# Attention units of 16 blocks, four exponentials in a row, and moved weight loads in a fused attention and feed-forward layer on eight cores

## The reference

```python
xn = _layernorm(x)                                  # x: 8 x 2048 x 1024
q, k, v = split(xn @ W_attn + b_attn)               # 16 heads of 64
att = q @ k.T / sqrt(64) / temperature + slope[h] * (pos_k - pos_q)   # causal
y = softmax(att) @ v
attn = y @ W_proj + b_proj
gate = xn @ (w_gate / 127).T                        # 3072 wide
up = xn @ (w_up / 127).T
ffn = (silu(gate) * up) @ (w_down / 127).T
out = x + attn + ffn
```

## Time and profile before

| | |
|---|---|
| median of 3 runs | 970.39 us (969.66 to 970.48) |
| the profiled execution | 968.67 us |
| its span on the slowest core (core 3) | 967.1 us (cores 958.5 to 967.1) |
| TensorE busy (x6272) | 905.9 us, 94% |
| VectorE busy | 498.7 us, 52% |
| ScalarE busy | 503.1 us, 52% |
| GpSimd busy | 300.5 us, 31% |
| mean granted TensorE clock, core 3 | 0.987 |

### The profile page before, as it was taken

The page is one execution under the profiler, slowest core; times in us unless marked ns, Lnnn a source line. Parts: engine busy times, 40 slices in busy tenths (PEclk is TensorE's granted clock), DMA queues, the critical chain, the costliest instruction groups (busy, mean ns, idle before and its releaser), DMA issues.

```text
span 967.1 us, 18777 instructions; the slowest of 8 cores (958.5 to 967.1 us)
## 1 busy us (share of the span) xinstructions
PE 905.9 (94%) x6272; PEld 407.4 (42%) x6272; DVE 498.7 (52%) x1110; ACT 503.1 (52%) x603; POOL 300.5 (31%) x296
## 2 busy tenths in 40 slices
PE   3999999999999999999999999979937999999998
PEld 1444344444444444444444444434413444444443
DVE  4650577777777777777777777766201011110111
ACT  3754677776787787787776877666323100000000
POOL 1010233323432324233324233345624233211220
PEclk9999999999999999999999999989978999999999
DMA  8842279999999999999899999999997837352221
GB/s 259 263 139 81 52 147 234 183 204 219 211 212 208 177 221 220 198 225 211 155 225 202 193 204 200 199 219 216 277 308 247 269 103 263 107 190 72 87 87 43
DMA packets 333341, 182.15 MB, mean 188 GB/s; under 512 B 303680, under 2 KB 315968, under 8 KB 329664
## 3 DMA queue, kind: packets, MB, share of 16 engines
q1 hardware_dynamic: 327776, 164.13, 76.2%
q0 software_dynamic: 2304, 8.39, 2.8%
q10 hardware_dynamic: 3168, 8.44, 2.3%
HBM read 84.46 MB, written 20.97 MB: 109 GB/s over the span
## 4 chain that ended last, share of the span: by engine, by line
PE 76%; DMA 6%; issue 6%; SPq 5%; DVE 4%; ACT 2%; POOL 1%; DVEq 0%; ACTq 0%; POOLq 0%
PE ps_r L911 25%; PE ps_dn L1003 17%; PE ps_r L894 11%; PE ps_s L963 7%; PE ps_dn L1010 6%; PE ps_y L978 5%; PE ps_r L934 4%; DMA xstage<-xin 3%; DMA late_i<-wd_r 2%; DVE sc L670 2%; SPq L388 2%; ACT pr L824 1%; SPq L471 1%; DVE st L617 1%; DMA stage_i<-wd_r 1%
## 5 line engine op out<-in xcount | busy, mean ns | idle before, releaser
L824 ACT ACTIVATE pr<-sc,cm 128x2048 bf16<-128x2048 f32 (+15 forms) x256 | 290.7, 1197 | 57.4 <-DVE cm L670 57.3
L670 DVE CUSTOM_DVE_ANT_0 sc<-ps_s,ramp 128x1024 f32<-128x1024 f32 (+7 forms) x256 | 243.8, 988 | 95.3 <-PE ps_s L963 80.5
L911 PE MATMUL ps_r<-xnT,wubuf 128*128 128x512 bf16 x768 | 206.9, 384 | 18.0 <-ACT gh_s L747 15.3
L911 PE MATMUL ps_r<-xnT,wgbuf 128*128 128x512 bf16 x768 | 204.8, 381 | 1.4 <-ACT gh_s L747 1.4
L1003 PE MATMUL ps_dn<-wdres,hb 128*128 128x512 bf16 x768 | 169.5, 381 | 5.0 <-DVE hst L698 5.0
L548 POOL TENSOR_SCALAR th_s<-th_s 128x512 f32<-128x512 f32 x96 | 59.3, 617 | 289.0 <-ACT th_s L745 288.9
L670 DVE CUSTOM_DVE_ANT_0 sc<-ps_s,ramp,cm 128x1024 f32<-128x1024 f32 (+7 forms) x128 | 99.9, 815 | 54.1 <-PE ps_s L963 53.5
L721 DVE SCALAR_TENSOR_TENSOR outsb<-ps_dn,xres 128x512 f32<-128x512 f32 x32 | 20.7, 687 | 202.9 <-PE ps_dn L1010 182.3
L894 PE MATMUL ps_r<-xnT,wqk_b 128*128 128x512 bf16 x512 | 120.9, 380 | 0.3 <-ACT gh_s L747 0.3
L554 POOL TENSOR_TENSOR gs_s<-th_s,gh_s 128x512 bf16<-128x512 f32 x96 | 111.2, 1159 | 26.2 <-POOL th_s L548 24.0
L1003 PEld LDWEIGHTS ps_dn<-wdres,hb 128*128 128x128 bf16 x768 | 75.4, 98 | 97.0 <-issue 7.4
(11 more groups left out here) (48 smaller groups left out, 530.7 us busy)
## 6 DMA issues: line engine op xcount, KB each, us to landing
stage_i<-wg_r SPq DMA_DIRECT2D x24, 512.0 KB, 4.6
stage_i<-wu_r SPq DMA_DIRECT2D x24, 512.0 KB, 5.6
h_sc<-hst SPq DMA_DIRECT2D x96, 128.0 KB, 2.4
late_i<-wd_r SPq DMA_DIRECT2D x9, 1024.0 KB, 9.0
hb<-h_sc SPq DMA_DIRECT2D x3, 3072.0 KB, 16.0
xstage<-xin SPq DMA_DIRECT2D x16, 512.0 KB, 6.5
stage_f<-wqk_r SPq DMA_DIRECT2D x8, 1024.0 KB, 6.1
xres<-xin POOLq DMA_DIRECT2D x16, 512.0 KB, 4.8
```

The lines of the kernel that those rows point to most:

```text
L670: e.tensor_tensor_reduce(scores(n, g + (2 if b == 2 else 0), c0, w), ps_s[:, g * 1024:g * 1024 + w], ramp[:, T - wide + c0:T - wide + c0 + ...
L824: e.activation(pr[n % 3][:, b0 * 128:(b0 + blocks) * 128], scores(n, r, 0, blocks * 128), AF.Exp, bias=cm[:, at:at + 1], scale=-1.0).then_ ...
L911: mm = e.matmul(ring(what, f), w[:, dc * 128:(dc + 1) * 128], xnT[:, dc * T + tb * 512:dc * T + tb * 512 + 512], start=(dc == 0), stop=(dc ...
```

## The change

It does five things.

1. **Units.** A pair has nine units instead of eight: (14,0), (13,1), ... (8,6) with 16 blocks a head, then row 15 alone (16 blocks) and row 7 alone (8 blocks). A unit has two steps of 1024 keys: the first 1024 of the long row, then the rest of the long row together with the short row in one filling of `ps_s`; row 7 has one step. That is 17 steps a pair instead of 24.
2. **ScalarE.** All four exponentials of a unit stand at the very start of ScalarE's work for the unit's last step, ahead of the Q or K copy and of the tanh of the gate products that end in that step.
3. **Weights.** The chain is split in two: gate and up through `stage_i`, and Q, K and the early down chunks, in halves of 512 KB, through `stage_f` and `stage_d`. Both stay in SyncE's queue.
4. **The end.** 92 pairs lie in the steps and 4 follow. h is collected in five `hst` buffers instead of four; the load of h for the first four row blocks and the first three late chunks are issued earlier; the late weights and the h block exchange their places in SBUF, and the three first late chunks all go to ScalarE behind the tanh of the last three gate products.
5. **The start.** Five small VectorE instructions on constants move from before the third to behind the fifth block of x; the first Q and K weights get a buffer of their own.

The core of the diff:

```diff
-NU = 8 * NHP
+UNITS = [(14 - j, j) for j in range(7)] + [(15,), (7,)]
+NUP = len(UNITS)
+NU = NUP * NHP
-NF_ATT = 88
+NF_ATT = 92
+NHS = 5
...
+    i, j = rows
+    return [[(0, 0, 1024)], [(0, 1024, (i - 7) * 128), (1, 0, (j + 1) * 128)]]
...
-    n, b = divmod(k, 3)
+    n, b = STEPS[k]
     n -= LAG
-    return [[(n, 0)], [(n, 1), (n, 2), (n, 3)], []][b]
+    rows = [(n, r) for r in range(2 * len(UNITS[n % NUP]))]
+    if b == 0 and not last_of(k):
+        return rows[:1]
+    return rows[1:] if b else rows
...
             for k in range(NST):
-                if k < NSB and qk_at(k) is not None:
+                n, b = STEPS[k]
+                if k < NSB and last_of(k):
+                    for r in range(2 * len(unit_of(n)[2])):
+                        weights(n, r)
+                if qk_at(k) is not None:
                     evac_qk(*qk_at(k))
                 for f in ended(k, "g"):
                     tanh_gate(f)
-                if k < NSB and k % 3:
-                    for r in range(2):
-                        weights(k // 3, r + (0 if k % 3 == 1 else 2))
...
             for f in ended_late("g"):
                 tanh_gate(f)
-                if f == NF_ATT + t:
-                    convert_late(t)
-                    t += 2
+                if f >= NF - 3:
+                    convert_late(f - NF + 3)
...
             for i in range(4, NT + 1):
...
+                if i == 5:
+                    e.wait_ge(sem["l_const"], 16 * 4)
+                    e.tensor_scalar(t8_s[:, :], temp_s[:, :], 8.0, None, AluOpType.mult).then_inc(sem["v_t"], 1)
```

More of the change, by code:

```diff
@@ new lines, in y_at, with y_block, batches_of @@
+def y_at(x):
+    return sum(len(rows) for rows in UNITS[:x])
+def y_block(tt):
+    return [i for rows in UNITS for i in rows].index(tt)
+def batches_of(x):
+    rows = UNITS[x]
+    if rows == (15,):
+        return [[(0, 0, 1024)], [(0, 1024, 1024)]]
+    if rows == (7,):
+        return [[(0, 0, 1024)]]
+    i, j = rows
+    return [[(0, 0, 1024)], [(0, 1024, (i - 7) * 128), (1, 0, (j + 1) * 128)]]
+STEPS = [(n, b) for n in range(NU) for b in range(len(batches_of(n % NUP)))]
+NSB = len(STEPS)
@@ new lines, with last_of @@
+STEPS += [(n, b) for n in range(NU, NU + LAG) for b in range(2)]
+NST = len(STEPS)
+def last_of(k):
+    return k + 1 == NST or STEPS[k + 1][0] != STEPS[k][0]
+SUMS = [(k, seg, g) for k in range(NSB) for seg in range(len(batches_of(STEPS[k][0] % NUP)[STEPS[k][1]]))
+        for g in range(2)]
+SUM_AT = {what: o for o, what in enumerate(SUMS)}
+ROW_AT = {}
+for _k, _seg, _g in SUMS:
+    _n, _b = STEPS[_k]
+    ROW_AT[_n, 2 * batches_of(_n % NUP)[_b][_seg][0] + _g] = SUM_AT[_k, _seg, _g]
+EXPS = [(n, r) for n in range(NU) for r in range(2 * len(UNITS[n % NUP]))]
@@ L200, in extra_loads, with late_done @@
 def extra_loads():
-    out = {}
+    items = {}
     for p in range(2, NHP):
[L205 to L209, removed]
+        f = FM[FIRST_OF[NUP * (p - 2)]] // 16 + 1
+        f += (1 - f) % 4
+        items[f], items[f + 2] = ("q", p, 0), ("q", p, 1)
+    f = FM[FIRST_OF[NUP * (NHP - 1)]] // 16 + 1
+    f += (1 - f) % 2
     for c in range(3):
-        out[f + 4 * c] = ("d", c)
-    return out
+        items[f + 4 * c], items[f + 4 * c + 2] = ("d", c, 0), ("d", c, 1)
+    return items
 EXTRA = extra_loads()
[L218 to L241, removed]
+EXTRAS = [("q", 1, 0), ("q", 1, 1)] + [EXTRA[f] for f in sorted(EXTRA)]
+NEARLY = sum(1 for what in EXTRAS if what[0] == "d") // 2
 NLATE = HCP - NEARLY + 4
+LATE_ON = ["a", "a", "a"] + ["ga"[t % 2] for t in range(NLATE - 3)]
+def late_done(t):
+    return f"{LATE_ON[t]}_lw", LATE_ON[:t + 1].count(LATE_ON[t])
 def build_program(T):
@@ L329, in build_program @@
             sd = [sb(first, f"sd{i}", [128, 1], F32) for i in range(4)]
+            wq_f = sb(first, "wq_f", [128, 2048], F32)
             rs = [sb(first, f"rs{i}", [128, 1], F32) for i in range(4)]
-        sc = sb(st, "sc", [128, 2 * 17 * 128], F32)
+        sc = sb(st, "sc", [128, 2 * 16 * 128], F32)
+        with contextlib.ExitStack() as late:
+            hb0 = sb(late, "hb0", [128, HCN * 512], BF16)
+        pr = [sb(st, f"pr{i}", [128, 32 * 128], BF16) for i in range(3)]
         with contextlib.ExitStack() as late:
@@ L1030, in _ @@
                     for half in range(2):
+                        if hc == 0 and tt == 2:
+                            if half == 0:
+                                e.wait_ge(sem["v_y"], NU)
+                            else:
+                                e.wait_ge(sem["v_h"], NF)
                         down(tt, hc, half)
```

418 lines of the change are left out of this document (205 added, 213 removed), and 4 rows, old and new, of the table SEMS.

## The result

| | before | after |
|---|---|---|
| median | 970.43 us (969.66 to 971.13, 4 runs) | 1050.24 us (1045.61 to 1051.85, 4 runs) |
| ratio, 95% interval | | 1.0815 (1.0778 to 1.0851) |
| profiled execution, its slowest core | 967.1 us (core 3) | 1047.6 us (core 2) |
| TensorE busy / idle in that span | 905.9 / 61.2 us | 924.4 / 123.2 us |
| granted clock, that core | 0.987 | 0.956 |

The change costs 8%, 80 us. The direction was forecast, the size was not: 1015 us was said, and 1050 lies outside the range of 986 to 1034. All medians and ratios leave out the runs in which one die held a much lower granted clock than the other, and in e13 and e14, where cores 4 to 7 held 0.98 in every run, cores 0 to 3 are compared.

What follows compares the result with a forecast made beforehand. The order of TensorE's instructions was taken as the bound; -11.2 - 35.4 - 5.2 + 1 + 69.4 + 8.6 + 18 = +45.2 on the 970.4 us median gave 1015 us (own range 1003 to 1027, eight in ten 986 to 1034).

Steps and rivals of the forecast that it cites:

- ScalarE's exponentials first, +69.4: Attention: tanh behind four exponentials frees gate banks late, TensorE stands; 69.4 us lost (55 to 77).
- its 0.3 a place: Method's excess at two observed places of the kernel before; 0.3 x 24 taken from 76.6, leaving 69.4 us.
- the eleven places: Gate ends within three matmuls of the scores, bank wanted in the same step: TensorE waits 43.2 us in all.
- the thirteen: Places where a Q or K product heading the next step wants the gate's bank: 29.0 us in all.
- The place worked out as 4.5: Example gate product: bank wanted at T + 3.2, free at T + 7.7 us, so TensorE stands 4.5 us.
- The clock, +18, with 5.2 of before gone: Eleven long stalls each bring half clock, 1.65 us apiece, +18 (0 to 24); earlier clock losses of 5.2 us vanish.
- The rival "more": Waits of 2.3 to 2.5 us drop the clock too, narrow scores cost, down waits: 1027 to 1036 us, chance 0.10.
- The whole 35.4 us of before come off: TensorE's earlier waits in and after the attention, 16.7 + 11.1 + 5.0 + 2.6 us, all vanish: -35.4.
- The 14.0 at the end: TensorE's wait until 724.49 us, late chunks and SyncE's queue delaying a tanh; said to vanish, within the 35.4.
- the 5.0 for cm at 633: Wait in the attention put down to the single chain of weights; splitting the chain removes 5.0 us.
- VectorE's waits, +8.6: Up products' banks come free after sums and division; TensorE waits in eleven units, +8.6 us (3 to 12).
- The groups of scores, -11.2: Score groups in the attention fall from 24 to 17 a pair, 56 x 0.20 us: -11.2 (8 to 12).

Runs made afterwards that it cites:

- e13: e2 with five of the six early down-chunk half loads cut to 16 columns of 1024, same instructions and order: 942.1 us, ratio 0.9694.
- e14: e2 with one wait added: in a unit's last step ScalarE does nothing before the step's first sum is there: 952.3 us, ratio 0.9788.
- e12: Changed kernel with tanh and copy of the eleven longest-waited gates ahead of the four exponentials, all others behind: 981.6 us, ratio 1.0098.
- e10: Changed kernel with 22 unread matmuls of 248 columns ahead of each of the eleven longest-waiting gate products only: 1024.8 us, ratio 1.0555.
- e2: Changed kernel with the tanh of gates ending within a last step's first nine gate and up matmuls ahead of the exponentials, later ones behind: 942.7 us, ratio 0.9676.
- e3: Kernel before, with only the four exponentials of a unit put first in ScalarE's work for the unit's third step: 987.0 us, ratio 1.0141.
- e4: Changed kernel with unread matmuls, 22 ahead of each of eleven gate products and 10 ahead of thirteen shorter-waiting products: 1017.1 us, ratio 1.0455.

## Why the prediction was wrong

Its sum of +45.2 us, term by term against what the runs showed:

- **ScalarE's exponentials first, +69.4.** Right in mechanism, place and count: 78.2 us in 32 pieces of up to 4.5, where 25 to 35 of up to 4.2 were said. The sum before its 0.3 a place was taken off, 76.6, was nearly exact: 43.2 were worked out for the eleven places and 29.0 for the thirteen, and the rows have 43.9 and 29.4. The place worked out as 4.5 measured 4.38 as the profile counts idle time, and 4.54 from when the matmul could have begun (184.71) to 189.25; at the two places of before, too, 0.16 us of what the method was too high by lies in this way of counting. +9 us.
- **The clock, +18, with 5.2 of before gone.** This is the step that failed most. The net was +12.8 and the trace shows +26. Two parts of it were wrong. The eleven long waits were given 1.65 us each; e12 has 24.9 / 11 = 2.3, since behind several of them the clock stayed at 1.2 GHz for twice as long, as in 237.8 to 244.6; its own hold such a price, 0.17 x 20 = 3.4 us in the stretch of the one wait of 5.0. And the thirteen waits of 1.5 to 2.9 us were given nothing, by the earlier trace rows, where 2.44 us idle had left the clock alone; e12 and e10 show 7 us for them. The rival "more" had this mechanism, at 1027 to 1036 us with a chance of 0.10.
- **The whole 35.4 us of before come off.** Half right. The 14.0 at the end and the 5.0 at the start of down are gone; down begins at 823 us without a wait and ends 224 us later. But the 5.0 for cm at 633 "goes, since the single chain of weights is split" was argued and not counted: before, GpSimd stood 9.5 us there for a down chunk, and with the chain split it stands 13.0 us for one and TensorE waits 9.4 us at 754. With the 1.8 of these, 6.1 us for cm remain in all.
- **VectorE's waits, +8.6.** 13.4 + 0.4 in the trace, of which 7.6 are that place at 754; the rest, 6.2, is within 3 to 12.
- **The groups of scores, -11.2.** Right, 11.1 in e2.

Idle time comes to +62 where the steps gave +43.6 (the ScalarE places 8.8 of the 18, the wait at 754 and what was left for cm the rest), the clock to 13 more. These 31 us are what the forecast of +45 lacks against +80, up to some 3. Neither alone would have carried the sum to 1050: with the clock's 13 it would have been some 1028 us, with the idle time's 18 some 1034.

The bounds of the clock were too narrow for one reason. The price of a clock drop came from the earlier trace rows, two waits, and was read as a mark between 2.44 and 2.61 us. There is no such mark. In the changed kernel the waits of 2.10 us at 500 us dropped the clock on all eight cores and those of 2.10 at 584 on none, 2.05 at 401 on all, 2.65 at 447 and at 621 on none. In e10, where the long waits between are filled, six of eight cores drop at 2.10 us near 480. Over the eight cores of the changed kernel 86 of the 88 long waits have a stretch at half clock in or just behind them, and 44 of the 104 shorter ones, the 1.50 us at 350 on six cores among them.

The Trainium skill (TensorE: Matmul & The Clock Gate, Why this matters for your kernels) wants no idle gap above about 3 us. The trace agrees that the waits above it, here 3.4 to 4.5 us, make the clock fall (86 of 88); it has falls behind waits of 1.50 and 2.05 us as well, so the measurement decides against it as a safe limit. The same page (Part 1: The HAM clock gate) says that the watch over TensorE runs freely and is not set back by the kernel, so that the same work meets it at another point each time. That agrees with cores that part at the same wait, as the six of eight; it was at hand, and would have spoken for counting the short waits in part.

What was right beside this: the change does what it says, the direction, that VectorE and DMA share do not become the bound in the attention, and that the four exponentials ahead of the tanh are the loss. e2 shows the last: 107.6 us hang on them, more than the loss of 80, for the rest of the change gains some 30 us (973.4 to 942.7 on one chip).

## What to carry to other kernels

An engine that works in order should not take a long job first because it is the more urgent one, if the job can't begin yet: ScalarE stood 2 us for its sums with a 1 us job behind it that TensorE needed, and 4 us of exponentials then lay on top. Together this cost 107 us; the standing still alone cost some 4. What such an order costs is first a count of the places that it hits: seven in the kernel before, for 14 us (e3), and 32 here. Put the short job into the gap where it ends early, and behind the long one where it ends late.

Price the clock behind every wait of TensorE of some 1.5 us and more: eleven waits of 3.4 to 4.5 us, 43.9 together, cost 24.9 more, and the shorter ones, 33.4, cost 7.3 more (slowest cores). Where a wait can't be removed, filling it with matmuls that nobody reads gave back 33 of 80 us.

## What the runs showed of the hardware that was not expected

The length of one wait does not tell whether the clock falls: 2.05 us did on eight of eight cores at 401 us, 2.65 us on none at 447, and even 1.50 us on six at 350. The same wait, 2.10 us, did it on none of eight at 584 in the changed kernel and on all eight near 563 in e10. Behind the wait at 401 the clock stayed at 1.2 GHz through most of the matmuls that followed, 3.01 us for eight where 1.89 is usual. Matmuls of 248 columns into an otherwise unused part of a bank kept it at 2.4 GHz: the mean granted clock of the slowest core was 0.993 in e4 against 0.956. What tells the waits that drop it from those that don't was not settled.
